# Attention and gated feed-forward on one core: sums of exponentials, places of the weight sums, and scores from hi and lo parts

## What is computed

```
L   = q @ k.T  / 4            L_y = q @ k_y.T / 4
agg = sum(exp(clip(L_y, -15, 15)) * mask, keys) + 1e-6
r   = log(|L| + 1e-6) - log(agg + 1e-6)
w   = softplus(r) * mask
out = (w / (sum(w) + 1e-6)) @ v, then @ w_proj.T
x   = layernorm(x + out)
x   = layernorm(x + ffn(x))      # three ternary layers, 1024 wide, silu gate, gelu
```

## Time and profile before

| | us |
|---|---|
| median of 3 runs | 1399.82 |
| profiled execution, its own time | 1398.2 |
| its span, first to last instruction | 1396.4 |
| TensorE busy | 1280.9 (92%) |
| VectorE busy | 718.2 (51%) |
| ScalarE busy | 614.8 (44%) |
| GpSimd busy | 113.3 (8%) |

### The profile page before, as it was taken

One profiled execution on the slowest core, in us unless ns is written; L12 is line 12 of the kernel. 1 busy time (PEld: TensorE's weight loads), 2 busy tenths in 40 slices (PEclk: granted clock), 3 DMA queues, 4 the chain that ended last, 5 costly groups with the idle time before them and its releaser, 6 DMA issues.

```text
span 1396.4 us, 22945 instructions
## 1 busy us (share of the span) xinstructions
PE 1280.9 (92%) x8310; PEld 817.6 (59%) x8310; DVE 718.2 (51%) x1223; ACT 614.8 (44%) x810; POOL 113.3 (8%) x140
## 2 busy tenths in 40 slices
PE   5888999999898989977399999999999999999996
PEld 1433444434343434433278778787787878878785
DVE  2456777677676776566243532535326353353523
ACT  3566666666666666655042322323223241232411
POOL 1111121111111121110000000000000000000000
PEclk8999999999999999998589999999999999999998
DMA  2002222132122221000290000000000000000000
GB/s 74 16 16 69 92 75 77 60 102 78 60 90 90 90 71 57 1 31 31 70 331 15 16 15 15 30 15 19 11 15 30 15 30 0 15 30 15 30 0 16
DMA packets 31943, 66.89 MB, mean 48 GB/s; under 512 B 2848, under 2 KB 8608, under 8 KB 31904
## 3 DMA queue, kind: packets, MB, share of 16 engines
q1 hardware_dynamic: 31904, 66.35, 14.3%
HBM read 46.42 MB, written 19.92 MB: 48 GB/s over the span
## 4 chain that ended last, share of the span: by engine, by line
issue 50%; POOL 0%; DVE 0%; POOLq 0%; DVEq 0%
POOL f_rstd L809 0%; DVE f_res L816 0%; POOLq L909 0%; DVEq L821 0%; POOL f_minus_half L907 0%; POOLq L83 0%
## 5 line engine op out<-in xcount | busy, mean ns | idle before, releaser
L935 ACT ACTIVATE f_h_full<-f_layer_bank,f_scales 128x512 f32<-128x512 f32 x128 | 88.0, 687 | 354.8 <-PE f_layer_bank L1049 354.7
L500 DVE TENSOR_TENSOR w_ring<-score_banks,keep 128x1024 int32<-128x1024 int32 (+1 forms) x192 | 191.6, 1040 | 46.9 <-PE score_banks L649 46.9
L353 ACT ACTIVATE e_ring<-score_banks 128x1024 f32<-128x1024 f32 (+1 forms) x192 | 158.8, 879 | 122.8 <-PE score_banks L649 122.0
L1049 PE MATMUL f_layer_bank<-f_ha_hi,f_w_all 128*128 128x512 f32 x512 | 204.7, 400 | 2.7 <-DVE f_h_full L977 2.3
L1049 PE MATMUL f_layer_bank<-f_hb_hi,f_w_all 128*128 128x512 f32 x512 | 202.8, 396 | 0.0
L1049 PE MATMUL f_layer_bank<-f_ha_lo,f_w_all 128*128 128x512 f32 x512 | 202.1, 395 | 0.0
L1049 PE MATMUL f_layer_bank<-f_hb_lo,f_w_all 128*128 128x512 f32 x512 | 202.0, 395 | 0.0
L491 DVE TENSOR_SCALAR e_ring<-e_ring 128x2048 f32<-128x2048 f32 (+1 forms) x96 | 100.5, 1046 | 122.3 <-ACT e_ring L353 122.3
L360 ACT ACTIVATE w_ring<-w_ring 128x2048 f32<-128x2048 f32 (+1 forms) x96 | 156.8, 1633 | 8.6 <-DVE w_ring L500 8.3
L287 POOL TENSOR_SCALAR_AFFINE_SELECT e_ring<-e_ring 128x512 f32<-128x512 f32 (+1 forms) x96 | 78.5, 818 | 516.5 <-DVE e_ring L491 516.5
L675 PE MATMUL acc_bank<-w_ring,v_aug 128*32 128x512 f32 (+3 forms) x1024 | 91.2, 452 | 27.8 <-ACT w_ring L360 27.8
(11 more groups left out here) (101 smaller groups left out, 1535.0 us busy)
## 6 DMA issues: line engine op xcount, KB each, us to landing
piece<-in_wf SPq DMA_DIRECT2D x44, 256.0 KB, 2.9
wf_copy<-piece SPq DMA_DIRECT2D x44, 256.0 KB, 3.0
f_w_all<-wf_copy SPq DMA_DIRECT2D x2, 4096.0 KB, 26.4
f_x_turn<-x SPq DMA_DIRECT2D x9, 512.0 KB, 3.2
xq<-in_xt SPq DMA_DIRECT2D x8, 512.0 KB, 3.3
xv<-in_xt SPq DMA_DIRECT2D x8, 512.0 KB, 3.3
res<-in_xn SPq DMA_DIRECT2D x8, 512.0 KB, 4.6
x<-res SPq DMA_DIRECT2D x8, 512.0 KB, 2.6
```

The lines of the kernel that those rows point to most:

```text
L353: nc.scalar.activation(e_ring[:, t % RING, 2 * i:2 * i + 2, 0:cols], pair_banks(y_pair(t, i), cols), ACT.Exp).then_inc(exp_done, 1)
L500: nc.vector.tensor_tensor(w_ring[:, t % RING, 2 * i:2 * i + 2, 0:cols].bitcast(I32), pair_banks(w_pair(t, i), cols).bitcast(I32), keep[:, ...
L935: nc.scalar.activation(h_full[m % 2][:], f_bank[m % RING][:], ACT.Gelu, scale=scales[:, 1 + layer, m:m + 1]).then_inc(gelu_done, 1)
L1049: mm = nc.tensor.matmul(out, left.bitcast(dt), right.bitcast(dt), start=first and n == 0, stop=last and n == 1)
```

## The change

It does three things, all in the attention phase.

- **Exponentials.** `e_ring` goes. The exponentials of the first of three beats are written to `e_sum` (two of them, one for each group of heads), those of the other two to `e_more`. GpSimd, after its mask, adds them to `e_sum` (`add_keys`, L310), tile by tile. TensorE then sums each group of three beats at once (`sum_exps`, L743), in beats 1 and 4.
- **Sums of the weights.** They now stand two beats behind and ahead of the w scores. `copy_sums` moves from beats 0 and 3 to beats 1 and 4, and several uses of `misc` change places with the w scores.
- **Scores.** q, qc, ky and k are split in hi and lo parts of type fp32r. ScalarE writes the hi parts, VectorE the lo parts (`lo_of`, L522), and each score set is three products, hi by hi, lo by hi and hi by lo, accumulated in the bank (L716).

```diff
-        def sums_of(t, y, w, before):
+        def beat_back(k, t, n):
+            return (k, t - n) if t >= n else (k.shift(-1), BEATS + t - n)
...
+            def add_keys(k, t):
+                added = 3 * quad_of(k, t) + (0, 0, 2)[t % CHUNKS]
+                reach(pool, e_masked, y_beat(k, t) + 1)
+                for n, (at, j) in enumerate(CHUNK_TILES[t % CHUNKS]):
+                    reach(pool, e_added, added + n)
+                    queries = e_sum[:, t // CHUNKS, :, P * j:T]
+                    nc.gpsimd.tensor_tensor(queries, queries, exps_of(t)[:, :, at:at + T - P * j], ALU.add).then_inc(e_added, 1)
...
-                nc.scalar.mul(q[0][u.half][:], misc[:], in_quad[:, 0:1]).then_inc(q0_made, 1)
+                for g in range(2):
+                    nc.scalar.mul(q_hi[g][u.half][:], misc[:], q_scale[:, g:g + 1])
+                nc.scalar.mul(q_full[u.half][:], misc[:], HD ** -0.5).then_inc(q_hi_made, 1)
+            def qc_halve(v):
+                reach(act, qc_full_made, v.index + 1)
+                reach(act, w_scores, BEATS * (v.index - 1))
+                for g in range(2):
+                    nc.scalar.mul(qc_hi[g][v.half][:], q_full[v.half][:], in_quad[:, g:g + 1]).then_inc(qc_hi_made, 1)
...
+            def lo_of(lo, hi, whole, scale):
+                return nc.vector.scalar_tensor_tensor(out=lo[:], in0=whole[:], scalar=scale, in1=hi[:].bitcast(F32),
+                                                      op0=ALU.mult, op1=ALU.subtract)
...
                 reach(dve, spread_ready, v.index + 1)
+                nc.vector.tensor_tensor(q_full[v.half][:], misc[:], q_full[v.half][:], ALU.mult).then_inc(qc_full_made, 1)
+            def qc_halve(v):
                 reach(dve, w_scores, BEATS * (v.index - 1))
                 for g in range(2):
-                    nc.vector.tensor_tensor(qc[g][v.half][:], misc[:], q[g][v.half][:], ALU.mult).then_inc(qc_made, 1)
+                    reach(dve, qc_hi_made, 2 * v.index + g + 1)
+                    lo_of(qc_lo[g][v.half], qc_hi[g][v.half], q_full[v.half], in_quad[:, g:g + 1]).then_inc(qc_made, 1)
...
             def scores(t, pair, left, right):
+                (lh, ll), (rh, rl) = left, right
                 for at, j in CHUNK_TILES[t % CHUNKS]:
-                    for r in range(QUAD):
-                        mm = nc.tensor.matmul(score[:, 2 * pair(t, r // 2) + r % 2, at:at + T - P * j],
-                                              left[lanes(r), P * j:P * j + P], right[lanes(r), P * j:T], start=True, stop=True)
+                    for n, (lt, rt) in enumerate(((lh, rh), (ll, rh), (lh, rl))):
+                        for r in range(QUAD):
+                            mm = nc.tensor.matmul(score[:, 2 * pair(t, r // 2) + r % 2, at:at + T - P * j],
+                                                  lt[lanes(r), P * j:P * j + P], rt[lanes(r), P * j:T], start=n == 0, stop=n == 2)
...
+            def sum_exps(k, g, alone):
+                reach(pe, e_added, 3 * (2 * k.index + g + 1))
+                if alone:
+                    reach(pe, acc_copied, 2 * k.index + g)
+                for r in range(QUAD):
+                    mm = nc.tensor.matmul(acc[lanes(r), :], sum_exp[:], e_sum[:, g, r, :], start=alone, stop=True)
+                mm.then_inc(e_summed, 1)
```

More of the change, by code:

```diff
@@ L306, in slot @@
                         mask_e(k, t)
+                    if y and t % CHUNKS:
+                        add_keys(k, t)
                     if t == 0 and norm is not None:
@@ L411, in slot @@
                 for t in range(BEATS):
-                    sums = sums_of(t, y, w, before)
+                    last, m = beat_back(k, t, 1)
                     if y:
@@ L436, in slot @@
                         piece_halve(k, t)
-                    if t == 0 and any(before):
-                        copy_sums(k.shift(-1), 1, before)
-                    if t == CHUNKS and (y or 0 in w):
-                        copy_sums(k, 0, (y, 0 in w))
             natural_order(0)
@@ L659, in scores_y @@
                 reach(pe, abs_done, 2 * m - 1)
[L660 removed]
+                scores(t, y_pair, (ky_hi[k.half], ky_lo[k.half]), (q_hi[t // CHUNKS][k.half], q_lo[t // CHUNKS][k.half])).then_inc(y_scores, 1)
             def scores_w(k, t, y):
@@ L668, in scores_w @@
                 reach(pe, exp_done, 2 * n + 1 if y else BEATS * UNITS * 2)
-                scores(t, w_pair, key[u.half], qc[at // CHUNKS][u.half]).then_inc(w_scores, 1)
-            def sum_keys(t, ring, stationary, first, last):
+                scores(t, w_pair, (key_hi[u.half], key_lo[u.half]), (qc_hi[at // CHUNKS][u.half], qc_lo[at // CHUNKS][u.half])).then_inc(w_scores, 1)
+            def sum_exps(k, g, alone):
[5 more added lines that the diff above has]
+                mm.then_inc(e_summed, 1)
@@ L673, in sum_keys, with sum_weights @@
+            def sum_weights(k, t, last):
+                u, m = weights_of(k, t)
+                first = t % CHUNKS == 0
+                reach(pe, ln_done, w_beat(k, t) + 1)
+                reach(pe, v_made, u.index + 1)
+                if first:
+                    reach(pe, acc_copied, 2 * k.index + t // CHUNKS)
                 for at, j in CHUNK_TILES[t % CHUNKS]:
                     for r in range(QUAD):
-                        mm = nc.tensor.matmul(acc[lanes(r), P * j:T], stationary(j, r), ring[:, t % RING, r, at:at + T - P * j],
-                                              start=first and t % CHUNKS == 0, stop=last and t % CHUNKS == CHUNKS - 1)
@@ L751, in slot @@
                 for t in range(BEATS):
-                    sums = sums_of(t, y, w, before)
-                    last = beat_before(k, t)
                     if y:
@@ L757, in slot @@
                         sum_values(k.shift(-1))
+                    if t == 1 and out is not None:
+                        turn(out, 1)
+                    if t == 2 and out is not None:
+                        project_out(out, 0)
+                    if t == 3 and out is not None:
+                        project_out(out, 1)
+                    if t == 4 and project:
+                        q_proj(k.shift(1))
+                    if t == 5 and y:
+                        v_proj(k)
+                    summed, m = beat_back(k, t, 2)
+                    exps_too = before[0] if t == 1 else t == 4 and y
+                    if weights_in(t, w, before):
+                        sum_weights(summed, m, m % CHUNKS == CHUNKS - 1 and not exps_too)
+                    if exps_too:
+                        sum_exps(summed, m // CHUNKS, not weights_in(t, w, before))
+                    if t in w:
+                        scores_w(k, t, y)
+                    if t == 0 and out is not None:
+                        turn(out, 0)
                     if t == 1 and any(before):
@@ L761, in slot @@
                         spread_c(k.shift(-1))
-                    if t == 3 and out is not None:
-                        project_out(out, 1)
+                    if t == 3 and project:
+                        ky_proj(k.shift(1))
                     if t == 4 and (y or 0 in w):
```

171 lines of the change are left out of this document (88 added, 83 removed).

## The result

| | before | after |
|---|---|---|
| median of the runs (us) | 1399.63 (4 runs) | 1539.38 (4 runs) |
| lowest to highest | 1397.06 to 1400.56 | 1538.31 to 1540.35 |
| span of the profiled execution | 1396.4 | 1538.6 |
| mean granted clock | 0.972 | 0.919 |
| TensorE, VectorE, ScalarE, GpSimd busy | 1280.9, 718.2, 614.8, 113.3 | 1286.6, 838.1, 651.8, 348.2 |

The change is slower by a ratio of 1.1005 (95% interval 1.098 to 1.1029), that is 140 us. The forecast was 1463 us, slower by 63, with a range up to 1495: right in its sign, wrong by 76 us and outside its range. All the time lies in the attention phase: the first product of the feed-forward layers starts at 860.0 us instead of 717.8, and from there to the end both take 678.6 us.

What follows compares the result with a forecast made beforehand. TensorE's load sets the even slot and short waits show in the odd; after the change, waits decide. Profiled 1398.2 us, +38 for beat waits, +25 for clock falls: 1461, as a median 1463; range 1420 to 1495.

Steps and rivals of the forecast that it cites:

- TensorE's load: Attention slots: fewer sums of exponentials and shorter score sets take 4 us off TensorE per slot, 64 us over 16.
- First and second beat: Attention slot's first two beats: 7.3 us, before 6.5, and 5.6 us, before 7.0 in the odd slot.
- Fourth beat: Dearest attention beat: w scores wait for qc's low parts behind the clip; 8.3 us, before 5.8 in the odd slot.
- The ledger as a whole: Six beat lengths summed: even slot 42.3 us, odd 40.7; +38 us over 16 attention slots.
- GpSimd then has 18 of 40 us and is read two beats later: hidden: Attention slots: GpSimd's additions, 11.6 us more a slot, cost no time.
- The rival of the ports: GpSimd's additions hold VectorE's next clip after the second beat: some 1.4 us a slot, +22, 1485 us; chance 0.15.
- Additions "in proportion": GpSimd's additions, scaled from a 1024-element multiplication of 1.93 us, take 11.6 us more a slot.
- The clock: Longer TensorE waits in attention bring 20 clock falls, between 0.6 and 1.7 us each, taken at 1.2: +25 us.
- The rival of the load: Fourth beat: qc's low parts come before the exponentials, w scores don't wait; 1336 or 1355 us; chance 0.1.

Runs made afterwards that it cites:

- the order alone: The change with fp32 scores (no hi and lo parts) and GpSimd additions of two columns, so only its order is left: 1403.62 us.
- the two-column run: The change with GpSimd's additions shortened to two columns of each head, their order, waits and releases kept: 1486.86 us.
- the run with spare additions: The kernel before, with GpSimd additions of the change's sizes behind the masks, on tiles that nobody reads: 1420.30 us.

## Why the prediction was right or wrong

**TensorE's load: right.** A set of 512 columns at full clock is 0.90 us (the w scores at 290.18 of the even slot, to the transpose at 291.08), 0.9 predicted for 1.07; with the order alone a pair has 6.5 us less to do, 6.2 predicted; and the load didn't decide.

**First and second beat: right** to 0.1 us, in both slots. **Fourth beat: right in its place.** The w scores did wait behind the clip, and moving the low parts one beat up gave 41 us. The ledger as a whole, +38 us, can be set beside the two-column run: its slots of 44.2 and 44.5 us at a clock of 0.96 and 0.92 come to 42.4 and 40.9 at full clock (an estimate, as if all of a slot went with the clock), with 42.3 and 40.7 predicted.

**"GpSimd then has 18 of 40 us and is read two beats later: hidden": this is the step that failed.** I asked only who reads the additions, not what they keep from running. 52 us of the change hang on their length, direct and by the clock.

**The rival of the ports: the right mechanism at the wrong instruction.** It spoke of the clip after the second beat, and in the middle of the phase no clip of the change was held (1.23 and 0.69 us as before). Before 90 us, and once at the end of the phase, seven were, by 11 us together, the longest just as the rival had it, behind the second beat:

```profile
63.36 3.92 DVE L545 TENSOR_SCALAR e_more<-e_more 128x1024 f32<-128x1024 f32 x1
```

In the other slots c's copy stood between. It came first, took the wait itself (3.08 us, and in the third beat TensorE waits for it) and so kept the clip clear of the additions; then the compares were held. At 22 us I had priced less than half of it. The Trainium skill, SBUF — State Buffer, on who interferes with whom, says that a VectorE instruction with two SBUF inputs contends with GpSimd's reads as one in a two-port mode does, and one with at most one SBUF input outside these modes does not. The rows agree in every case above. I had read it for the clip only, and not held each VectorE instruction of the slot against it.

**Additions "in proportion": too short.** 1024 elements take 2.37 us, not 1.93, in the change as on spare tiles (2.36). VectorE is not the reason: the additions at 137.29 and 185.15 us, with no VectorE instruction over them, took 2.37 as well. The row I scaled from multiplies by a broadcast operand; whether that is why it's faster was not tried. With 1.28 and 3.45 for the other two it makes 14.2 us a slot instead of 11.6.

**The clock: right in kind, too small.** I took 20 falls at 1.2 us, +25. Filling the two waits of odd slots gave 15 us back, some 2 for each such slot; the even slots have falls as well (0.89) and weren't tried, so that the whole price in the change is an estimate only: some 30 us, if they lose as much. The two-column run gives another: without any hold its pairs still take 88.7 us where the ledger has 83.0, 5.7 a pair or 46 us over eight, and by the estimate above the clock accounts for them. That is 21 us more than the 25 taken; with the 52 us of the additions' length it makes 73 of the 76 us that were missing. The wait at the spread (2.14) comes from a hold, and so the failed step fed this one. The wait at the w scores (3.44) doesn't: it is 4.2 us in the two-column run, and 3.5 was predicted.

**The rival of the load (faster, 0.1): wrong for this order**, yet the whole change does get below the kernel before once the low parts and the additions are placed for it, though not below that kernel with its own queues reordered.

## What to carry to other kernels

Work moved to GpSimd is hidden only if no VectorE instruction with two SBUF operands, and none that copies, scales or clips within SBUF, stands where it runs: go through the queue of VectorE over the length of each GpSimd instruction, and read held ones off their own durations, not off idle time. Place instructions that read PSUM there, or cut the GpSimd instruction so that a hold is short. And when a change costs a fixed order much, try the order before dropping the change: here the same work took 1539 and 1392 us. Then give the kernel before the same treatment, or the gain of the new order is put down to the change: here 17 us (1398.3 to 1381.1) came without any change of the work.

## What the runs showed of the hardware

- A held VectorE instruction waits for the end of the GpSimd instruction that runs, whatever its own size. In the run with spare additions, the operation on four elements for the variance had a mean of 1.12 us instead of 0.17, and the one on 64 elements for the denominators 1.49 instead of 0.25.
- Not held over additions: the absolute values (PSUM and SBUF, 1.217 us), q's low part (PSUM, 0.746), bn_stats (0.41) and a reciprocal of 64 elements within SBUF (0.55).
- The hold works both ways and also with the mask: with qc's low parts under way the mask of 512 elements took 0.852 us instead of 0.677, and the low parts 0.95 instead of 0.70, also with two-column additions (0.860 and 0.954).
- A score set of 512 columns in four row groups took 0.90 us as three products of rounded parts, and 1.07 as one fp32 product, which has two instructions in each row group.
- 30 transposes in each odd slot that nobody reads made the kernel 15 us faster, with the mean clock at 0.944 instead of 0.919 and nothing else changed.
